# A graph neural network's five steps on one core: a dense count matrix and gathered rows against slots of 32 edges, expanded and placed by column-tiled products

## The reference

```
h = max(layernorm(x), 0)
row, col = src, dst
def step(h):
    messages = h[col] @ W_msg.T + b_msg
    agg = segment_sum(messages, row, num_segments=12500)
    gi = agg @ W_ih.T + b_ih
    gh = h @ W_hh.T + b_hh
    r = sigmoid(i_r + h_r)
    z = sigmoid(i_z + h_z)
    n = tanh(i_n + r * h_n)
    return (1 - z) * n + z * h
out = x + step applied five times to h
```

## Time and profile before

| | us |
|---|---|
| median of 3 runs (5293.96 to 5297.8) | 5296.72 |
| span of the profiled execution, first to last instruction | 5295.2 |
| TensorE products busy | 4969.6 (94%) |
| POOL busy | 3751.4 (71%) |
| VectorE busy | 2590.3 (49%) |
| ScalarE busy | 861.8 (16%) |
| mean granted TensorE clock | 0.975 |

### The profile page before, as it was taken

How to read it: one execution, slowest core, us unless ns; L and a number is a source line. 1 busy time by engine, 2 the same in 40 slices (tenths; PEclk the granted TensorE clock), 3 DMA queues, 4 the chain that set the end, 5 groups by cost and what they waited for, 6 DMA issues and landing times. The chain is left out here.

```text
span 5295.2 us, 80372 instructions
## 1 busy us (share of the span) xinstructions
PE 4969.6 (94%) x26501; PEld 2539.4 (48%) x26502; DVE 2590.3 (49%) x6993; ACT 861.8 (16%) x1421; POOL 3751.4 (71%) x3869
## 2 busy tenths in 40 slices
PE   5588888699999699999999999999999999999998
PEld 1344444355555345555555555555555555555554
DVE  8899993356666633433333433333343333333332
ACT  7666662000000000000000000000000000000000
POOL 3777777777776777677777677777767777757774
PEclk7799999899999799999999999999999999999999
DMA  5255555466666466666676666666666667566654
GB/s 170 68 165 164 164 165 167 118 183 183 175 174 173 114 195 182 185 181 181 176 203 179 183 180 181 180 188 192 178 184 181 181 179 212 177 182 188 189 177 125
DMA packets 1036729, 916.12 MB, mean 173 GB/s; under 512 B 507905, under 2 KB 771453, under 8 KB 1036412
## 3 DMA queue, kind: packets, MB, share of 16 engines
q1 hardware_dynamic: 482262, 661.95, 40.1%
q0 software_dynamic: 123920, 212.72, 15.0%
q10 hardware_dynamic: 430358, 39.09, 6.0%
HBM read 766.27 MB, written 147.15 MB: 172 GB/s over the span
## 5 line engine op out<-in xcount | busy, mean ns | idle before, releaser
L696 POOL DMA_INDIRECT f_ring<-fast_hrows,f_work x3175 | 3070.9, 967 | 1208.7 <-issue 950.6
L990 PE MATMUL f_ps_a<-f_ring,f_hr 128*128 128x512 fp8e4 (+1 forms) x13560 | 3017.1, 375 | 6.9 <-DMA f_ring<-fast_adj 6.9
L990 PEld LDWEIGHTS f_ps_a<-f_ring,f_hr 128*128 128x128 f16 x13560 | 1308.2, 98 | 1473.8 <-issue 138.2
L1500 DVE TENSOR_SCALAR f_ring<-f_iota_h,f_work 128x128 f16<-128x128 f16 (+1 forms) x3175 | 614.0, 283 | 1026.8 <-PE f_ps_a L1002 984.8
L674 POOL DMA_INDIRECT fast_rec<-f_slots x656 | 645.1, 983 | 213.7 <-issue 199.6
L1002 PE MATMUL f_ps_a<-f_ring 128*128 128x128 f16 (+1 forms) x5726 | 542.7, 237 | 62.9 <-DMA f_ring<-fast_hrows,f_work 62.7
L1424 DVE SCALAR_TENSOR_TENSOR f_work<-f_deg,f_bias_c,f_ps_c 128x512 f32<-128x512 f32 x125 | 93.5, 748 | 1009.8 <-PE f_ps_deg L1029 1009.8
L1002 PEld LDWEIGHTS f_ps_a<-f_ring 128*128 128x128 f16 x5726 | 440.8, 98 | 260.8 <-DMA f_ring<-fast_hrows,f_work 68.1
L792 ACT ACTIVATE f_work<-f_work,f_bsum 128x512 f32<-128x512 f32 x125 | 90.2, 722 | 2223.4 <-DVE f_work L1424 2223.4
L1374 DVE TENSOR_SCALAR f_ring<-f_iota_h,f_work 128x256 f16<-128x256 f16 x1536 | 413.2, 373 | 0.0
L949 PE MATMUL f_ps_deg<-f_ring,f_sel 128*128 128x512 fp8e4 x1536 | 395.6, 381 | 0.0
(11 more groups left out here) (322 smaller groups left out, 3164.3 us busy)
## 6 DMA issues: line engine op xcount, KB each, us to landing
f_ring<-fast_adj SPq DMA_DIRECT2D x750, 640.0 KB, 4.2
fast_adj<-f_ring SPq DMA_DIRECT2D x192, 512.0 KB, 3.2
f_ring<-fast_hrows,f_work POOLq DMA_INDIRECT x3175
f_deg<-fast_deg SPq DMA_DIRECT2D x125, 256.0 KB
fast_hrows<-f_work ACTq DMA_DIRECT2D x400, 64.0 KB
f_hr<-fast_hrows SPq DMA_DIRECT2D x24, 640.0 KB, 7.1
fast_rec<-f_slots POOLq DMA_INDIRECT x656, 2.4
fast_hrows<-f_deg SPq DMA_DIRECT2D x1, 6528.0 KB, 39.4
```

Source lines behind the costliest of these rows:

```text
L696: nc.gpsimd.indirect_dma_start(G[:, g * 2 * H:(g + 1) * 2 * H], None, hrows, bass.IndirectOffsetOnAxis(ap=idx_tab[:, col + g:col + g + 1], ...
L990: mm = pe.matmul(sumT[buf][:, 0:cols], lhsT=hr[:, t, a * H:(a + 1) * H], rhs=a_f8[:, t * CHUNK:t * CHUNK + cols], start=(t == 0 and a == 0 ...
L1500: ins = nc.vector.tensor_scalar(OH[:, g * HALF:g * HALF + w], iota_h[:, 0:w], loc[:, bass.ds(col + g, 1)], HOT, ALU.is_equal, ALU.mult)
```

## The change

The fast program is written anew. A chunk is now 256 nodes, 49 of them, 245 in five steps; x has 98 tiles of 128 rows.

**Slots.** The edges between one tile of 128 source nodes and one tile of 128 destination nodes (a block) get up to 32 slots. Four source tiles make a group, so a group has 128 slots for each of the chunk's two destination tiles, and a chunk has 25 groups. For each chunk two tables of 128x6400 bytes are built in the setup and stored in DRAM (`adj_e`, `adj_o`): E has for each slot a one-hot of 8-bit floats over the tile's 128 source rows, O for each slot a one-hot over 128 destinations. Edges past slot 32 of a block, up to 128 a chunk, are gathered as before, one indirect DMA a chunk.

**Expand, copy, place.** For each group `expand` multiplies E by the kept rows: 32 slots of a tile as weights, the tile's row halves (256 columns) as moving data, the result in 32 of 128 partitions of a PSUM bank, so that the four tiles' products fill the four quarters of the array's columns. ScalarE (two groups of three) or VectorE (one of three) copies the 128x512 result to SBUF as f16 (`Gx`). `place` multiplies O by it, again as four products with 32 rows of output each, and adds to a second bank. The four products of `place` have the same moving data.

**Rows on chip.** `hr` now holds all 98 tiles twice, for this step and the next. The new h is transposed and its halves are written straight into the next step's copy (`new_rows`); nothing is loaded again. Rows are still stored to DRAM for the gather.

**Setup.** The count matrix and its build, the scatter of records and the second way for 4820 nodes go. All edges are now keyed, ranked and put into tables, in two halves (912 and 950 columns): 49 key products and 49 masked copies for each half, then 50 pieces of one-hots with up to 80 column-tiled products of 49 columns each, then table operations. In the build each chunk's E comes from 50 products of 128 columns and absolute differences (seven units of up to 1024 columns, three on VectorE and four on ScalarE), its O from two operations of 1600 elements on VectorE; SP stores both. Degrees are summed from O.

The core of the diff (the rest renames, frees or moves what these need):

```diff
-                def dense(t, buf, cols):
-                    for a in range(2):
-                        mm = pe.matmul(sumT[buf][:, 0:cols], lhsT=hr[:, t, a * H:(a + 1) * H], rhs=a_f8[:, t * CHUNK:t * CHUNK + cols],
-                                       start=(t == 0 and a == 0), stop=(t == T1 - 1 and a == 1), skip_group_check=True)
-                    return mm
...
+                def expand(n, ph, s, g):
+                    buf = X[(ph + g) % RING]
+                    e = e8[ph % 2]
+                    for u in range(2):
+                        k = 2 * g + u
+                        for j in range(4):
+                            mm = pe.matmul(buf[32 * j:32 * j + 32, u * CW:(u + 1) * CW], lhsT=e[:, k * P + 32 * j:k * P + 32 * j + 32],
+                                           rhs=hr[:, s % 2, min(4 * g + j, NT - 1), :], start=True, stop=True, skip_group_check=True)
+                    mm.then_inc(expanded, 1)
+
+                def place(n, ph, g):
+                    evacuated(pe, n, g)
+                    if g == 0:
+                        pe.wait_ge(hr_ready, n + 1)
+                    pe.sem_inc(pe_turns, 1)
+                    kept = Gx[(ph + g) % RING]
+                    o = o8[ph % 2]
+                    for u in range(2):
+                        k = 2 * g + u
+                        for j in range(4):
+                            pe.matmul(R[ph % 2][32 * j:32 * j + 32, u * CW:(u + 1) * CW], lhsT=o[:, k * P + 32 * j:k * P + 32 * j + 32],
+                                      rhs=kept[:, u * CW:(u + 1) * CW], start=(g == 0 and u == 0), stop=False, skip_group_check=True)
...
+                    for g in range(NG):
+                        if begun and g == 5:
+                            turn_sums(m, r)
+                            gates_of_h(m, c)
+                        if begun and g == 8:
+                            gates_of_sum(m)
+                        if begun and g == 21:
+                            turn_rows(m, r)
...
+                        expand(n, ph, s, g)
+                        if g >= LAG:
...
+                            place(n, ph, g - LAG)
...
+                    for g in DVE_G:
+                        evacuate(n, ph, g)
...
+                        if g == 19:
+                            new_h(m)
+                            if sp_ < STEPS - 1:
+                                new_rows(m, cp, sp_, r)
```

More of the change, by code:

```diff
@@ L151, in build_fast @@
[L151 to L170, removed]
@@ L195, in two @@
[L195 to L217, removed]
@@ new lines, in build_fast, with words @@
+        ring = sb("ring", [P, 12832], I32)
+        def words(at, count):
+            return ring[:, at:at + count]
+        eb = [words(a * EW // 4, EW // 4) for a in range(2)]
+        ob = [words((2 + a) * EW // 4, EW // 4) for a in range(2)]
+        e8 = [t.bitcast(F8) for t in eb]
+        o8 = [t.bitcast(F8) for t in ob]
+        at = EW
+        Gx = [words(at + a * CW, CW).bitcast(F16) for a in range(RING)]
+        at += RING * CW
+        G = [words(at + a * P, P).bitcast(F16) for a in range(2)]
@@ L452, in build_fast @@
-        assert all(len(windows(cls, g)) in (1, 2) for cls in RANGES for g in range(TILES[cls]))
-        def number(cls, s, k):
-            if is_ahead(cls, s, k):
-                return k
-            return s * NCH + k + {"A": ahead("A", s, k), "B": NA + ahead("B", s, k), "C": NA + 1}[cls]
-        def chunk_of(cls, k):
-            return {"A": k + C1, "B": NCH - 1, "C": k}[cls]
-        def first_chunk(s):
-            return ("C", 0) if s == 0 else ("A", 0)
-        def starts(cls, s, k):
-            return isinstance(k, int) and (cls, k) == first_chunk(s)
@@ new lines, in _ @@
+            for c in range(NCH):
+                for v, (first, end) in enumerate(UNITS):
+                    n = c * len(UNITS) + v
+                    if n >= 3:
+                        cp, vp = (n - 3) // len(UNITS), (n - 3) % len(UNITS)
+                        if vp in DVE_U:
+                            pe.wait_ge(e_built_dve, cp * len(DVE_U) + DVE_U.index(vp) + 1)
+                        else:
+                            pe.wait_ge(dist_ready, cp * len(ACT_U) + ACT_U.index(vp) + 1)
+                    for k in range(first, end):
+                        at = (k - first) * P
+                        mm = pe.matmul(pairs[n % 3][:, at:at + P], lhsT=locd[:, c * SLOTS + k:c * SLOTS + k + 1].to_broadcast([P, P]),
+                                       rhs=ident_h[:], start=True, stop=True)
+                    mm.then_inc(spread, 1)
+                if c > 0:
+                    add_degrees(c - 1)
```

1929 lines of the change are left out of this document (844 added, 1085 removed).

## The result

The changed kernel takes 6249.33 us (median of 4 runs, 6236.04 to 6261.12) against 5297.2 us for the kernel before beside it: 1.180 times, with a 95% interval of 1.178 to 1.181. I had forecast 5080. The profiled execution has a span of 6246.6 us.

A forecast was written before the change was run, and what follows sets the result against it. TensorE streaming columns without a pause was taken to bound the steps, behind a setup with other owners. Forecast: 1020 us setup + 4042 for 245 chunks + 18 tail = 5080 us, a gain of 4%, range 4640 to 6300.

The forecast's parts named there:

- the sum of 16.5 us a chunk: Steps: 14.1 us of TensorE products plus 2.4 of waits for VectorE and ScalarE; 245 chunks make 4042 us.
- that no issue limit has shown yet: TensorE in the steps: load and product pairs of every width cost only their columns, so a set was taken at 0.109 us.
- Sets side by side: Expanding and placing: four products run together in the array's quarters, 0.109 us a set, 102 sets 11.1 us a chunk.
- The rival of sets short of four: Steps: loads of 32 columns not hidden, a set 0.123 to 0.165 us; at 0.140 the kernel takes 5595; chance 0.22.
- pairs hold at 0.055: Rival, steps: load and product pairs start no faster than 0.055 us, a set 0.222, the kernel 7460 us; chance 0.12.
- the wait for the new h: Steps, TensorE's group 21: TensorE waits for VectorE to make the new h before turning it, 1.2 us a chunk.
- the 1.2 us for ScalarE's gates: Steps, groups 14 to 17: gate functions delay ScalarE's copies, so TensorE waits about 1.2 us a chunk.
- Changes of arrangement: Steps: entering and leaving the tiled arrangement six times a chunk, priced between nothing and 0.165 us each, up to 1.0.
- Clock: Steps: TensorE stands 2.4 of 16.5 us, yet its granted clock stays at 1.00; costed at nothing.
- Transfers: Steps: tables, rows and gathers need 112 GB/s against 179 now; TensorE waits for tables only if SP is over 10 us late.
- Setup: Before the steps: 555 us, then 441 of build and 20 of flags; steps begin at about 1020 us, bounds 960 and 1150.
- some stall that I haven't seen: Remaining rival, steps: an unseen stall, or the four products of a set running one after another; chance 0.06 together.

The follow-up runs named there:

- the cut loop: Changed kernel with two chunks a loop, some placing by whole products and 49 empty instructions ahead of the loops of steps 2 to 5: 5522.11 us, 1.043 times before.
- the run with small tables: Changed kernel, loading only the first 512 of 6400 bytes a row of each chunk's two tables: 5929.41 us, 1.120 times before.
- the loop of 1812: Changed kernel with two chunks instead of four in the loop of the steps, placing still in quarters: 6117.52 us, 1.156 times before.
- the run with whole products alone: Changed kernel, four chunks a loop, placing by one product of 128 weight columns instead of four of 32: 6476.15 us, 1.223 times before.
- the short loop: Changed kernel with two chunks a loop and, where the 0.66 us a group was read, placing by whole products too: 6178.77 us, 1.166 times before.

## Why the prediction was wrong

I gave "faster" 0.55; the kernel is 18% slower.

*The step that failed* is the sum of 16.5 us a chunk: it adds columns and two waits for other engines and puts the bringing of TensorE's instructions at nothing. The reason that stands nearest, "that no issue limit has shown yet", was read from a loop of 780 instructions that stayed on the chip. The changed loop has 3620, and neither the sum nor a named rival asked where instructions come from. The runs put the fetches at about 4.0 us a chunk (20.9 against 16.95 in a round without one), some 970 us of the miss of 1169. The rest is 84 us of setup and some 110 us by which a round without a fetch is longer than 16.5 us a chunk. The page of before had the hint: its instruction queue moved 1.61 MB in all, and the diff tells the number of products.

*Sets side by side*: right, 0.11 us, not 0.12 to 0.17. The rival of sets short of four, with the Trainium skill's rule on column tiling ("TensorEngine Tiling (Array Packing)", Restrictions) and the ratio of 2.38 behind it, isn't borne out for loads of 32 columns under products of 256: the trace has four starts in 0.11 us. Neither did pairs hold at 0.055.

*The sum of a chunk*: nearly right for a loop that stays. Rounds without a fetch take 33.3 to 33.7 us in the cut loop (outside the first step, with its table loads), 16.7 a chunk, against 16.5. That is in part luck, for its parts were less even: the wait for the new h was 1.2, as placed, and 1.0 came back when it was moved; the 1.2 us for ScalarE's gates were not there (in the changed kernel placing waits 28.6 us in all for ScalarE's copies); in their place stand short waits for the turned sums, about 0.3 a chunk, and the changes of arrangement, which the sum had left out.

*Changes of arrangement*: I bounded six of them by 0 to 1.0 us. At 0.11 each they are 0.7, inside.

*Clock*: costed at nothing, 1.00 forecast. It was 0.95 in the steps and 0.99 once the stalls were gone. These rows (columns as in rows 2) end and begin at the gap of 4.23 us above:

```profile
2000.00:2016.00 16.00, 14.31 (x374) 11.23 (x364) 9.72 (x21) 8.88 (x18) 0.94 (x1) 1.00 0.33 114
2016.00:2032.00 16.00, 11.77 (x226) 9.35 (x218) 4.20 (x9) 6.22 (x11) 0.94 (x1) 0.79 0.39 126
```

From 1.00, the level of 2.4 GHz, it fell to 0.79 in the mean, so that a part of the second stretch ran at 1.2 GHz. The clock follows the stalls, though not each of them: the long round of 40.8 us above kept 1.00 with gaps of up to 3.8 us.

*Transfers*: the bandwidth was enough, as said, 98 GB/s. But the run with small tables is 320 us shorter, with the same number of instruction packets: the transfers add to the stalls. I had looked for a wait for a table only.

*Setup*: 1104 against 1020, inside the bounds of 960 to 1150. The build begins at 580 instead of 555 and takes 10.2 us a chunk instead of 9, as the first units of two successive chunks on VectorE show:

```profile
802.60 1.28 DVE L1118 TENSOR_SCALAR f_ring<-f_ps_a,f_cols 128x1024 uint8<-128x1024 f32 x1 [2.48 <-PE f_ps_a L743]
...
812.82 1.28 DVE L1118 TENSOR_SCALAR f_ring<-f_ps_b,f_cols 128x1024 uint8<-128x1024 f32 x1 [2.48 <-PE f_ps_b L743]
```

VectorE waits 2.48 us in each for TensorE's products of 128 columns, at a clock of 0.82. The one-hot pieces take 2.4 us, as costed.

*The numbers*: "some stall that I haven't seen" had 0.06 together with the four taking turns; this is that stall. The time lies inside the range, near its end, by luck: the range's end was drawn for sets of 0.174 us.

What stays open: at what length, to the instruction, a loop stops staying. Loops of 780 and 1190 stayed, 1692 in seven blocks stayed or nearly so, 1692 and 1812 in eight were fetched in every second round or in all, 2370 and 3620 in each. In the loop of 1812, which lies over eight blocks in all five steps, two steps fetch in every round and three in every second, so the number of blocks alone doesn't decide; nor does the place alone, since the cut loop had long rounds where the same loop with the new h turned later had none. What the fetches and the changes of arrangement each cost in the run with whole products alone is not shown, for no time is read from its trace; its packets and the 0.66 us a group of the short loop say only that it has both.

## What to carry to other kernels

Count instructions as well as columns: when an edit splits products, multiply them by the number of rounds, look at the instruction queue of the page, and ask whether the loop's body still stays on the chip. If gaps without a releaser ("issue") of a microsecond or more stand ahead of an engine's densest instructions and repeat every 256 of them, shorten the loop's body before changing the work in it. A narrow product is worth its columns only next to others of its kind, since each change to the whole array costs a tenth of a microsecond.

## What the runs showed that I had not expected

The same loop of 1692 instructions takes 5363 or 5922 us by where it lies: 66 empty instructions fewer ahead of it, executed once, put it over eight blocks of 256 instead of seven. Rounds that fetch and rounds that don't alternate within one execution (33.9 and 40.8 us), so a mean over chunks hides them. A change between quarters of the array and the whole of it costs 0.22 us there and back. And a loop that is entered with another ScalarE table than it ends with loads tables in each round, 2 x 1.28 us, in one step of five: 47 us.
